# Moving the three bf16 casts of each batch's keys from ScalarE to GpSimd in a cross-attention stage, and expert ids from 32 to 16 bits

## What is computed

```
q = x @ Wq + bq;  kv = context @ Wkv + bkv;  k, v = split(kv)
q = _larope(q, Lq);  k = _larope(k, Lk)          # rotation by position
scores = einsum('bhqd,bhkd->bhqk', q, k) * SCALE # 16 heads of 16 channels
attn = softmax(where(mask, scores, -inf))
out = einsum('bhqk,bhkd->bhqd', attn, v) ...  @ Wo + bo
```

## Time and profile before

| | |
|---|---|
| median of 3 runs | 2003.54 us (2001.28 to 2003.62) |
| span of the profiled execution | 2002.3 us |
| PE busy in the span | 1765.5 us (88%) |
| DVE busy | 1442.3 us (72%) |
| ACT busy | 1052.5 us (53%) |
| POOL busy | 993.1 us (50%) |
| mean granted TensorE clock | 0.962 of full |

### The profile page before, as it was taken

One profiled execution on the slowest core, in us unless ns is written; L12 is line 12 of the kernel. 1 busy time (PEld: TensorE's weight loads), 2 busy tenths in 40 slices (PEclk: granted clock), 3 DMA queues, 4 the chain that ended last, 5 costly groups with the idle time before them and its releaser, 6 DMA issues. The chain is left out here.

```text
span 2002.3 us, 33243 instructions
## 1 busy us (share of the span) xinstructions
PE 1765.5 (88%) x11070; PEld 1108.0 (55%) x11070; DVE 1442.3 (72%) x2729; ACT 1052.5 (53%) x2220; POOL 993.1 (50%) x740
## 2 busy tenths in 40 slices
PE   7957887889889999898799999997899989998799
PEld 4433444444567676644444444444744746665699
DVE  6768999995578888758676766664754367886893
ACT  4776667672588887734665655664322231114342
POOL 1269889892462222004577777775000028664342
PEclk9979999999899999999899999998989989999799
DMA  2033443332576656240166665734830053435540
GB/s 72 0 124 110 138 138 127 121 129 80 120 170 157 160 142 161 68 142 24 44 217 213 204 194 169 238 96 130 265 99 1 17 168 116 136 123 179 197 133 17
DMA packets 138159, 257.43 MB, mean 129 GB/s; under 512 B 30661, under 2 KB 94822, under 8 KB 135318
## 3 DMA queue, kind: packets, MB, share of 16 engines
q1 hardware_dynamic: 120358, 212.16, 35.5%
q0 software_dynamic: 13824, 37.77, 6.2%
q10 hardware_dynamic: 3808, 5.38, 1.1%
HBM read 205.82 MB, written 49.44 MB: 127 GB/s over the span
## 5 line engine op out<-in xcount | busy, mean ns | idle before, releaser
L2355 POOL TENSOR_TENSOR soft_power<-soft_logit,soft_high 128x1024 f32<-128x1024 f32 x28 | 66.2, 2363 | 290.8 <-DVE soft_high L2429 290.5
L3211 PE MATMUL moe_up_ps<-moe_w_tile,ahead 128*64 128x352 f32 x1152 | 193.5, 480 | 0.9 <-issue 0.7
L3148 POOL DMA_INDIRECT moe_y<-ahead,moe_where x144 | 157.3, 1092 | 64.4 <-issue 38.7
L3355 ACT ACTIVATE moe_w_tile<-moe_w 128x1216 f32 x144 | 175.1, 1217 | 20.5 <-issue 19.0
L1791 ACT ACTIVATE xattn_prob<-xattn_sm,xattn_least 112x375 f32<-112x375 f32 x256 | 155.0, 606 | 53.5 <-DVE xattn_least L1692 48.7
L1692 DVE CUSTOM_DVE_ANT_0 xattn_sm<-xattn_s_ps,wide 112x375 f32<-112x375 f32 x256 | 137.7, 542 | 53.3 <-PE xattn_s_ps L1574 30.3
L3142 POOL DMA_INDIRECT ahead<-moe_tok,moe_where x144 | 147.4, 1024 | 57.0 <-issue 42.1
L1584 PE MATMUL xattn_pt_ps<-ident,xattn_prob 112*125 112x112 f32 x768 | 131.3, 280 | 24.0 <-ACT xattn_pt L1797 13.5
L1584 PEld LDWEIGHTS xattn_pt_ps<-ident,xattn_prob 112*125 112x125 f32 x768 | 112.9, 190 | 63.9 <-ACT xattn_prob L1791 43.2
L1023 POOL TENSOR_TENSOR mamba_x_state<-mamba_x_state,mamba_cx_all 128x896 f32<-128x896 f32 x64 | 133.7, 2088 | 26.0 <-DVE mamba_x_state L1081 25.9
L1017 POOL TENSOR_TENSOR xn<-mamba_u,mamba_b_all 128x896 f32<-128x896 f32 x64 | 133.6, 2090 | 14.9 <-DMA mamba_b_all<-mamba_b 14.9
(11 more groups left out here) (454 smaller groups left out, 4279.6 us busy)
## 6 DMA issues: line engine op xcount, KB each, us to landing
moe_w<-moe_w SPq DMA_DIRECT2D x64, 480.0 KB, 3.8
soft_w<-soft_w SPq DMA_DIRECT2D x16, 1024.0 KB, 7.1
mamba_b_all<-mamba_b SPq DMA_DIRECT2D x32, 448.0 KB
mamba_cx_all<-mamba_c SPq DMA_DIRECT2D x32, 448.0 KB, 3.8
mamba_cy_all<-mamba_c SPq DMA_DIRECT2D x32, 448.0 KB, 4.7
moe_w_tile<-moe_y SPq DMA_DIRECT2D x14, 1024.0 KB, 7.6
soft_logits<-soft_logit SPq DMA_DIRECT2D x28, 512.0 KB, 2.6
soft_logit<-soft_logits SPq DMA_DIRECT2D x14, 1024.0 KB, 5.1
```

The lines of the kernel that those rows point to most:

```text
L3148: pool.indirect_dma_start(y_dram, bass.IndirectOffsetOnAxis(ap=where[:, 1, t:t + 1], axis=0), y_sb[:, 2 * s + i], None).then_inc(y_stored[ ...
L3211: mm = pe.matmul(up_ps[n * HALF:(n + 1) * HALF, i, 0:2 * I], xT[:, s % 2, at:at + HALF], w_tile[:, s, i, n, h * 2 * I:(h + 1) * 2 * I], st ...
L3355: place_weights = weight_placer(act, 0, lambda to, src: act.activation(to, src, ACT.Copy))
```

## The change

In cross-attention ScalarE no longer casts the keys. GpSimd does it, with a `tensor_copy` from fp32 to bf16 of the same 128 x 750 elements, straight behind the sum and behind each lessening; the waits are the same ones (`k_whole`, `k_less`, and the store of the part's previous content), and so are the counts that SyncE waits for. It holds for batches 1 to 15, in the stage's opening and in the loop. The expert ids become 16-bit unsigned integers in SBUF, in DRAM and in the register loads.

```
-            KEYS_AT, ROTATE_AT, CAST_AT = (0, 1, 2, 4), (2, 3, 5, 6), (8, 12, 15)
+            KEYS_AT, ROTATE_AT = (0, 1, 2, 4), (2, 3, 5, 6)
...
+                def cast_keys(b, n):
+                    if n == 0:
+                        pool.wait_ge(k_whole, b + 1)
+                    else:
+                        pool.wait_ge(k_less, (PARTS - 1) * b + n)
+                    wait(pool, k_stored[n], 16 * b)
+                    pool.tensor_copy(part[:, n], key[:]).then_inc(k_cast, 1)
...
                 sum_keys(1)
+                cast_keys(1, 0)
                 pool.wait_ge(q_whole, 2)
                 for n in range(PARTS - 1):
                     lessen_keys(1, n)
+                    cast_keys(1, n + 1)
                     lessen_queries(OTHERS, n)
                 for b in range(B - 2):
                     if b < NCH - 1:
                         turn_queries(OTHERS + 1 + b)
                     sum_keys(b + 2)
+                    cast_keys(b + 2, 0)
                     for n in range(PARTS - 1):
                         if b < NCH - 1:
                             lessen_queries(OTHERS + 1 + b, n)
                         lessen_keys(b + 2, n)
+                        cast_keys(b + 2, n + 1)
...
-                    act.activation(part[:, n], key[:], ACT.Copy).then_inc(k_cast, 1)
...
-                        if follows(b, 2) and h in CAST_AT:
-                            cast_keys(b + 2, CAST_AT.index(h))
...
                 keep_queries(4)
-                cast_keys(1, 2)
                 cast_queries(OTHERS, 2)
...
-    expert_dram = k.dram("moe_expert", [HR * P], I32)
+    expert_dram = k.dram("moe_expert", [HR * P], U16)
...
-        expert_row = k.sb(ctx, "moe_expert_row", [1, HR * P], I32)
+        expert_row = k.sb(ctx, "moe_expert_row", [1, HR * P], U16)
...
-            expert = sb("expert", [P, HR], I32)
+            expert = sb("expert", [P, HR], U16)
```

More of the change, by code:

```diff
@@ L16 @@
 I32 = mybir.dt.int32
+U16 = mybir.dt.uint16
 U8 = mybir.dt.uint8
@@ L1860, in _ @@
                 keep_queries(2)
-                cast_keys(1, 0)
                 cast_queries(OTHERS, 0)
@@ L1866, in _ @@
                 keep_queries(3)
-                cast_keys(1, 1)
                 cast_queries(OTHERS, 1)
```

## The result

The changed kernel takes 2047.78 us (median of four runs, 2041.01 to 2050.24) where the kernel before takes 2002.41 on the same chip: a ratio of 1.0222, 95% interval 1.0197 to 1.0247. Slower by 2.2%, where I had forecast 1999.5 us and a range up to 2010. I was wrong by 48 us, and not in one place.

| stage | before, us | after, us | difference |
|---|---|---|---|
| cross-attention | 344.9 | 357.5 | +12.6 |
| experts | 572.5 | 603.0 | +30.5 |
| all the rest together | | | about 0 |

The account below looks back on a forecast made before the run. Steady cross-attention batches were taken as bound by 15.70 us of TensorE work plus 4.38 us of context flight. Gains of -6.2 us and +2.2 us (-1.0 + 2.0 + 1.2) gave -4.0: 1999.5 us from the median, range 1994 to 2010.

Parts of the forecast that it names:

- Expert ids: Experts' register loads of 16 ids: -2 us if 16 bits halved them and one in four stood on the path; taken 0.
- The first two: Steady cross-attention batch: TensorE's 0.32 and 0.61 us waits for ScalarE, put down to its casts, worth nothing beside the context's flight.
- batch 13's -0.9: Cross-attention batch 13: no context load follows, so TensorE's waits for ScalarE count in full, -0.9 us.
- batches 1 and 2: Cross-attention batches with query work: freed of waits for ScalarE, their period falls to 19.7 us, -1.3 us each.
- batch 0: Cross-attention batch 0, ending on the context with the longest flight, 5.6 us: between 0 and 1.6 us less, taken -0.8.
- The half clock at 596 us: Behind batch 2's waits TensorE runs at 1.2 GHz from 596.4 to 599.8 us; gone as the wait shrinks, -1.2 us.
- The context: Ten gated cross-attention batches: key loads and third store share DMA engines with the context load, +0.2 us each, +2.0.
- The clock: Cross-attention batch ends: TensorE's waits become one of 1.6 us, bringing the low clock once in ten batches, +1.2 us.
- rival A: Cross-attention: key loads catch the context, landing 0.8 us later in ten batches, +8, clock +7; 2011 us; chance 22%.
- GpSimd, 1.1 us a cast: Cross-attention key casts on GpSimd: 1.1 us each, range 0.7 to 1.6, hidden in steady batches and in batches 0 to 2.
- Rival B: No change: at 1.6 us a cast GpSimd becomes the bound of cross-attention batches 0 to 2; 2003 us; chance 20%.
- Ten batches gated by the context: Cross-attention batches 4 to 13 start on the context's landing; its load issued 0.1 us sooner each, -1.0 us.

Follow-up runs that it names:

- after_again: The changed kernel measured once more (GpSimd casts, 16-bit ids): 2049.91 us, 1.0238 of the kernel before.
- ids16_again: The kernel before with only the expert ids in 16 bits, ScalarE still casting, a repeat run: 2040.35 us, 1.0199 of the kernel before.
- mask_only: The kernel before with each expert id masked to 8 bits before it is waited on, a control: 2075.10 us, 0.9988 of the kernel before.
- casts_store_held: casts_only with SyncE waiting, ahead of a batch's third key store, until the next batch's context has landed: 2001.35 us, 1.0003 of the kernel before.
- keys_late: mask_only with a batch's key projections after heads 1, 2, 3, 4 instead of 0, 1, 2, 4: 2005.60 us, 1.0021 of the kernel before.
- casts_again: casts_only once more, on a chip where the kernel before takes 2000.21 us: 2015.13 us, 1.0059 of the kernel before.
- casts_ctx_first: casts_only with SyncE holding only the key loads until the next batch's context has landed: 2079.80 us, 1.0012 of the kernel before.
- casts_only: The changed kernel with expert ids back in 32 bits, and masked to 8 bits before each wait: 2088.85 us, 1.0051 of the kernel before.

## Why the prediction was wrong, by its steps

- **Expert ids, "I take 0, range -2 to +1":** the chief failure, mis-sized by 30 us in the changed kernel's trace and by 38 in after_again's and ids16_again's. I let the size in bytes stand for the time of a register load, and bounded an operation of which the trace had one row, in 32 bits, on the side of gain only. Nothing in rows 13 excluded a loss, and I had no row of 16 bits. Nor had I read the 1.8 us of room behind the load, by which a longer one would have been priced: if all 18 had the room of that pair, 2.6 us longer less 1.8 is 14 us even without the clock. The waits came to 23.4 us, and the slower matmuls to 16.3.
- **"The first two are what the casts on ScalarE make or help to make":** false. The 0.32 and 0.61 us of rows 3 stand in the changed trace unaltered, before the matmuls at 677.63 and 678.97, and the waits for ScalarE are 20.5 us in all for 19.3. With them go batch 13's -0.9 and most of batches 1 and 2. The stretch from the first key matmul to that of batch 4 was 110.0 us before and 109.5 after; but traces with ScalarE's casts also have 107.4 and 107.5 (mask_only, ids16_again). By pieces, against the traces with ScalarE's casts: the opening is 1.0 us shorter (forecast 0.7), batches 1 and 2 together some 0.9 us shorter (20.7 and 20.2 us for 20.9 and 20.9; forecast 2.6), and batch 0, forecast 0.8 shorter, is 1.7 longer (23.0 us for 21.3, in the kernel before itself 22.2), with a half clock at about 552 us that all eight traces with GpSimd's casts have and none of the eight with ScalarE's. I had no term for that, and did not find its cause. The half clock at 596 us that I counted as the casts' (-1.2) is in two of the eight traces with ScalarE's casts: mostly it is absent with them too. casts_store_held shows the whole gain once the cost is off: 344.9 to 343.6 us, within what the traces with ScalarE's casts and the keys in their place show (342.4 to 344.9).
- **The context, "+0.2 each":** the mechanism was named right, including which transfers, and sized too small. From its issue to the signal of its landing the context takes 4.7 to 5.3 us on the mean of ten batches in the four traces with nothing held and the keys in place, for 4.0 to 4.2 with ScalarE's casts: 0.7 to 1.1 us later where I had 0.2. I had looked at when the key loads begin, and took the stores leaving early as relief; but the third store did about as much of the harm as the key loads (landing 5.2, 4.6 and 4.1 us). To be issued 0.6 us ahead of another transfer is no relief; the two stores 1.3 and 1.8 us ahead did no harm that shows.
- **The clock, "one case in ten batches at 1.2":** three in the changed kernel, 6.1 us; by rival A six were 7.
- **GpSimd, 1.1 us a cast:** 0.81, inside the range; hidden as said. Rival B did not come.
- **Ten batches gated by the context:** right but for one. In the kernel before, nine of the ten first key matmuls start within 0.05 us of the landing's signal, and that is why most of a microsecond counts ten times. The row I quoted for it I read wrongly: "5.4, 12" counts the waits of TensorE and of its weight loads apart, for the same groups; TensorE's own are 5, with 2.0 us. And I did not see how close the next limit lies: in keys_late, with no wait for the context, a batch takes 19.8 us.
- **Rival A** is what the cross-attention did: it gave +8 over the span with gains of 7.2, of which on balance nothing came, so +15 without them, and casts_again measured +14.9. Its terms were +8 for the transfers and +7 for the clock; the nine batches of the changed kernel show 6.5 and 6.5. I gave it 22%. In its own test ("median above 4.5") it is met by 4.7. The 30 to 38 us beyond were in no rival.

## What to carry to other kernels

An engine may be loaded, and be what the critical engine waits for beside a transfer, and still give nothing when it is relieved: ask which wait ends last, and check in a second trace that a half-clock stretch is the place's and not chance. Making a producer faster moves its stores forward, and they may fall on the load that the critical engine waits for; where one load gates every round, try tying the others to its landing. Change a type in memory only after looking for who reads it into registers, and price such a load by the room behind it in program order.

## What the runs showed of the hardware that I had not expected

- A register load (TENSOR_LOAD from SBUF) of 16 values takes 1.02 us on ScalarE and 1.10 on VectorE in 32 bits, 3.6 and 3.8 in 16 or 8 bits; of 8 values 0.55 and 0.60 in 32 bits, 1.73 and 1.85 in 16.
- A GpSimd cast of 128 x 750 from fp32 to bf16 takes 0.81 us, as long as ScalarE's 0.82.
- A 375 KB load lands in 4.0 to 4.2 us (medians) with ScalarE's casts; in 4.6 with a third store of small packets issued mostly 0.57 us ahead of it (casts_ctx_first); in 4.6 to 5.2 with the key loads issued from 2.2 us behind it as well (four traces).
- About half of that delay lies behind the load's last data packet: from there to the signal of the landing are 0.35 us on the mean before, 0.80 in the changed kernel, 0.90 in casts_only and 0.34 in casts_store_held.
- The kernel before takes 2000 to 2002 us in four of five groups of runs and 2078 in one, on a chip of its own; by mask_only's trace from there the difference stands in the experts' stage (648 us for 572).
